# A vision-transformer block on one core: half of a pair's embedding one step ahead, the front part's pieces one slot up, the stores spread, and the last expert in plain products

## The reference

```python
h = _L0_tok_ref(x, L0_tok_W, L0_tok_b)                       # patches (768) @ W.T + b + position
h = concatenate([cls_tok, h], axis=1)                         # 197 tokens
h = h + _L0_attn_ref(_layernorm(h), w_qkv, w_out, b_out)      # 16 heads of 16
h = h + _L0_ffn_ref(_layernorm(h), W1, b1, W2, b2, Wu, bu)

# attention weights: s = p(logits - row maximum), s / sum(s), p a rational function
# the experts (4, hidden size 1024), each token s:
u = sigmoid(x @ Wu + bu);  k = clip(ceil(u * 4), 1, 4)
y = relu(x @ W1[e] + b1[e]) @ W2[e] + b2[e]                   # for every e
out = sum over i = 1..4 of (u / i if k >= i else 0) * y[(s + i - 1) % 4]
```

## Time and profile before

| what | value |
| --- | --- |
| median of 3 runs | 4080.23 us (4076.17 to 4082.94) |
| the profiled execution | 4075.9 us, of which 4074.1 us are the span of its trace |
| PE busy | 3943.3 us, 97% |
| DVE, ACT, POOL busy | 2770.1, 2396.5, 2648.0 us |
| share of the chain that ended last | PE 74%, DVE 12%, issue 4%, DMA 4% |
| transfers | 407.50 MB, mean 100 GB/s |

### The profile page before, as it was taken

One profiled execution on the slowest core, in us unless ns is written; L12 is line 12 of the kernel. 1 busy time (PEld: TensorE's weight loads), 2 busy tenths in 40 slices (PEclk: granted clock), 3 DMA queues, 4 the chain that ended last, 5 costly groups with the idle time before them and its releaser, 6 DMA issues.

```text
span 4074.1 us, 84992 instructions
## 1 busy us (share of the span) xinstructions
PE 3943.3 (97%) x29760; PEld 3331.0 (82%) x29760; DVE 2770.1 (68%) x4223; ACT 2396.5 (59%) x4361; POOL 2648.0 (65%) x3437
## 2 busy tenths in 40 slices
PE   7899999999999999999999999999999999999997
PEld 4688888888888888888888888888888888888887
DVE  5666767667767667676667666677776676766752
ACT  5555566655666555666555665556665556655562
POOL 5466666656667666666566666666665666666677
PEclk8899999999999999999999999999999999999999
DMA  6233333333333333333333333333333333333333
GB/s 193 61 98 99 97 101 99 95 105 83 106 101 102 97 100 96 102 99 98 101 92 99 101 101 99 103 91 102 99 100 101 97 98 102 101 95 90 97 108 94
DMA packets 693839, 407.50 MB, mean 100 GB/s; under 512 B 149169, under 2 KB 684081, under 8 KB 692401
## 3 DMA queue, kind: packets, MB, share of 16 engines
q1 hardware_dynamic: 690400, 401.98, 34.7%
q10 hardware_dynamic: 3024, 0.09, 0.0%
HBM read 384.79 MB, written 17.10 MB: 99 GB/s over the span
## 4 chain that ended last, share of the span: by engine, by line
PE 74%; DVE 12%; issue 4%; DMA 4%; ACT 2%; POOL 2%; SPq 1%; DVEq 0%; ACTq 0%; POOLq 0%
PE ps L1148 45%; PE ps L1278 6%; PE ps L1246 5%; PE ps L1319 4%; PE ps L1231 4%; DMA w1s<-w_sums 4%; PE ps L1260 3%; DVE probs L843 2%; PE ps L1336 2%; DVE lows L916 2%; PE ps L1328 1%; DVE rt L887 1%; DVE rden L863 1%; DVE rstd L889 1%; ACT probs L611 1%
## 5 line engine op out<-in xcount | busy, mean ns | idle before, releaser
L1148 PE MATMUL ps<-xn,w1s 128*128 128x197 f32 x4096 | 903.1, 342 | 4.9 <-ACT hT L576 2.6
L1148 PE MATMUL ps<-hT,w_s 128*128 128x197 f32 x4096 | 790.4, 330 | 9.8 <-POOL hT L474 8.1
L1148 PEld LDWEIGHTS ps<-xn,w1s 128*128 128x128 f32 x4096 | 677.2, 189 | 138.7 <-issue 134.6
L1148 PEld LDWEIGHTS ps<-hT,w_s 128*128 128x128 f32 x4096 | 696.6, 190 | 13.3 <-issue 8.9
L474 POOL TENSOR_TENSOR hT<-hT 128x197 f32<-128x197 f32 x512 | 311.4, 608 | 608.1 <-ACT hT L591 603.2
L1148 PE MATMUL ps<-xt,w1s 128*128 128x197 f32 x3072 | 686.2, 332 | 18.8 <-DMA w1s<-w_sums 17.7
L843 DVE SCALAR_TENSOR_TENSOR probs<-probs,ps 99x788 f32<-99x788 f32 x512 | 481.1, 971 | 307.7 <-ACT probs L611 307.7
L467 POOL TENSOR_SCALAR hT<-hT 128x394 f32<-128x394 f32 x512 | 620.2, 1211 | 20.1 <-DVE hT L958 20.1
L1148 PEld LDWEIGHTS ps<-xt,w1s 128*128 128x128 f32 x3072 | 533.9, 189 | 105.9 <-issue 45.2
L916 DVE TENSOR_REDUCE lows<-ps 99x8 f32<-99x1576 f32 (+1 forms) x256 | 460.4, 1799 | 229.2 <-PE ps L1246 229.2
L1148 PE MATMUL ps<-hT,w_a 128*128 128x197 f32 x3072 | 601.5, 330 | 0.7 <-DVE yw L976 0.7
(11 more groups left out here) (113 smaller groups left out, 5945.8 us busy)
## 6 DMA issues: line engine op xcount, KB each, us to landing
w_a<-in_w SPq DMA_DIRECT2D x384, 256.0 KB, 3.1
w1s<-w_sums SPq DMA_DIRECT2D x512, 192.0 KB, 2.6
w1s<-in_w SPq DMA_DIRECT2D x512, 128.0 KB, 2.4
x<-in_xT SPq DMA_DIRECT2D x30, 1188.0 KB, 5.4
w1s<-in_w SPq DMA_DIRECT2D x512, 64.0 KB, 2.0
w1s<-w_sums SPq DMA_DIRECT2D x512, 64.0 KB, 2.0
out_rows<-rows SPq DMA_DIRECT2D x256, 48.0 KB
hT<-in_w SPq DMA_DIRECT2D x8, 1024.0 KB, 8.6
```

Source lines behind the costliest of these rows:

```text
L1148: return mm(place, weights, rows, start=start, stop=True, skip_group_check=True)
```

## The change

Five things are changed together.

1. **Half of the embedding one step ahead.** `embed(f, 0)` moves to the end of the step before, behind `gate_logit`, and `z` goes from bank 0 to bank `Y1`.
2. **The front's pieces one slot up.** On PE: `embed(f, 1)` in slot 0, `mean` in slot 1, `variance` in slot 2, q and k in slots 4 and 5, v in slot 6. On POOL: `sum_h` in slot 0 and `sum_squares` in slot 2. On ACT and DVE the pieces that go with them move too, and the order of `log_of`, `halves`, `whole`, `normal`, `up_sums_1` and `refine` around them is another. `weigh` goes to other gaps.
3. **The gate's reciprocal in two halves** (`sigmoid`, `sigmoid_2`), and `gate_sum` before the last `low`.
4. **Stores**: three in each of slots 8 to 11, behind the weights of the slot, in place of twelve in slot 9 before them.
5. **The end**: the last expert's down product is done in 16 plain products of 394 columns (`final_products`), with the weight block `a21` loaded to the free pixel buffer; DVE weighs, adds and transposes each half (`final_rows`), and SP and ACT store them by halves, 16 transfers.

```diff
@@ SP
-                    if s == 9 and has_t:
-                        store(t)
...
+                    if n == LAST and s == 8:
+                        sp.wait_ge(emb_done, 2 * PAIRS)
+                        sp.dma_start(a21[:], w2[E - 1][:, 0:COUPLES, P:2 * P]).then_inc(a21_in, 16)
+                    if 8 <= s < 12 and has_t and t < LAST:
+                        store(t, s - 8)
@@ POOL
-                    if s == 1 and has_f:
+                    if s == (1 if f == 1 else 0) and has_f:
                         sum_h(f)
-                    if s == 3 and has_f:
+                    if s == (3 if f == 1 else 2) and has_f:
                         sum_squares(f)
@@ ACT
                 relus(1)
+                if has_f:
+                    h_of(f, 0)
                 for k in range(8):
...
+                    if k == 3 and has_f:
+                        rs_of(f)
...
-                    if k in (0, 1) and has_f:
-                        h_of(f, k)
+                    if k == 0 and has_f:
+                        h_of(f, 1)
...
-                    if k == 2 and has_f:
+                    if k == 1 and has_f:
                         squares(f)
@@ DVE
+                    if k == 2 and has_f:
+                        spread(f, "var", var_done, vt_ready)
                     late(k)
+                    if k == 1 and has_f:
+                        centre(f)
                     if k == 1 and has_n:
                         sigmoid(n)
+                    if k == 2 and has_n:
+                        sigmoid_2(n)
...
+                    if k == 3 and has_f:
+                        refine(f, rs_ready, nt_ready, ht_ready, rstd_ready)
+                        normal_rows(f)
+                    if k == 3:
+                        even(4)
@@ PE
                 if has_b:
-                    gap(b, 0, (low_ready, at(b, 8, 8)), (zb_ready, at(n, 1, 1)), (q_max_ready, at(b, 4, 4)))
+                    gap(b, 0, (low_ready, at(b, 8, 8)), (zb_ready, at(n, 1, 1)), (q_max_ready, at(b, 4, 4)), *([(h_ready, at(f, 2, 1))] if has_f else []))
                 experts(1)
                 if has_f:
-                    embed(f, 0, read(1))
+                    embed(f, 1, read(1))
...
-                    embed(f, 1, read(3))
+                    mean(f, read(3))
...
-                    mean(f, read(5))
+                    variance(f, read(5))
...
                 if has_b:
-                    gate_logit(b, (low_ready, at(f, 8, 8)) if has_f else (vt2_ready, at(b, 1, 1)))
+                    gate_logit(b, (whole_ready, at(b, 8, 8)))
+                if pair + 2 < PAIRS:
+                    embed(pair + 2, 0, (low_ready, at(f, 8, 8)))
+
+            def final_products():
+                pe.wait_ge(a21_in, 16)
+                pe.wait_ge(poly_ready, at(PAIRS, 16, 0))
+                for m in range(DK):
+                    for g in range(COUPLES):
+                        c = FINAL * COUPLES + g
+                        pe.wait_ge(r1_ready, c + 1)
+                        mm(final_y(m), (w_a[:, 0, g], a21[:, g])[m], hidden(c), start=g == 0, stop=False)
+                        pe.wait_ge(r2_ready, c + 1)
+                        if g == 0:
+                            pe.wait_ge(wa_in[(1, 2)[m]], 16 * PAIRS * E)
+                        ins = mm(final_y(m), w_a[:, (1, 2)[m], g], hidden2(c), start=False, stop=g == COUPLES - 1)
+                    ins.then_inc(final_done, 1)
```

More of the change, by code:

```diff
@@ L317, in vit_block, with final_y, store_last @@
         STORES = 4 * (DK + 1)
+        LAST_STORES = 4 * DK * 2
+        FINAL = PAIRS * E - 1
+        a21 = x[:].rearrange("p a k s -> p (a k s)")[:, 0:COUPLES * P].rearrange("p (g c) -> p g c", g=COUPLES)
+        def final_y(m):
+            return ps[:, m, 0:N]
+        def store_last(eng, a, m):
+            eng.wait_ge(rows_ready, LAST + 1 + m)
+            to = out[LAST * N:(LAST + 1) * N, m * P + 32 * a:m * P + 32 * a + 32]
+            full = (NB - 1) * 32
+            eng.dma_start(to[0:full].rearrange("(j n) c -> n j c", n=32),
+                          rows[32 * a:32 * a + 32, m, 0:full].rearrange("p (j c) -> p j c", c=32)).then_inc(rows_out, 16)
+            eng.dma_start(to[full:N], rows[32 * a:32 * a + N - full, m, full:NROW]).then_inc(rows_out, 16)
         block = ctx.enter_context(nc.Block())
@@ L330, in store @@
                 full = (NB - 1) * 32
[L331 to L335, removed]
+                for m in range(DK):
+                    sp.dma_start(to[0:full, a, m, :].rearrange("(j n) c -> n j c", n=32),
+                                 rows[32 * a:32 * a + 32, m, 0:full].rearrange("p (j c) -> p j c", c=32)).then_inc(rows_out, 16)
+                sp.dma_start(to[full:N, a], rows[32 * a:32 * a + N - full, :, full:NROW]).then_inc(rows_out, 16)
             def load_x_part(c):
@@ L776, in step @@
                         square(b, k, 1)
-                    if k in (5, 7) and has_b:
-                        halves(b, (k - 3) // 2)
+                    if k in (6, 7) and has_b:
+                        halves(b, k - 5)
                     if k == 0 and has_n:
@@ L824, in _ @@
             run_steps(step)
+            for m in range(DK):
+                for a in range(2, 4):
+                    store_last(act, a, m)
         @block.vector
@@ L986, in y_weighted, with final_rows @@
                                                op0=ALU.add, op1=ALU.mult).then_inc(yw_ready, 1)
+            def final_rows():
+                dve.wait_ge(gate, at(LAST, 9, 9))
+                dve.wait_ge(rows_out, STORES * 16 * LAST)
+                for m in range(DK):
+                    part = h2[:, LAST % 2, m, 0:N]
+                    dve.wait_ge(final_done, m + 1)
+                    dve.wait_ge(y_ready, at(FINAL, 2, 0))
+                    nc.vector.scalar_tensor_tensor(out=two(yw[:, m, :]), in0=two(final_y(m)), scalar=b2s[:, E - 1, m:m + 1], in1=weight_of(E - 1),
+                                                   op0=ALU.add, op1=ALU.mult).then_inc(final_ready, 1)
+                    dve.wait_ge(final_ready, 2 * m + 1)
+                    nc.vector.tensor_tensor(part, part, yw[:, m, :], ALU.add).then_inc(final_ready, 1)
+                    dve.wait_ge(final_ready, 2 * m + 2)
+                    nc.vector.transpose(rows[:, m, :], h2[:, LAST % 2, m, :]).then_inc(rows_ready, 1)
             def rows_of_pair(t):
@@ L1080, in step @@
                         poly(b, k, 0)
-                    if k in (5, 7) and has_b:
-                        whole(b, (k - 3) // 2)
+                    if k in (6, 7) and has_b:
+                        whole(b, k - 5)
+                    if k in (3, 4, 7):
+                        odd_up(k)
                     if has_b:
                         poly(b, k, 1)
-                    odd(k)
+                    if k not in (3, 4, 7):
+                        odd_up(k)
+                    odd_down(k)
```

139 lines of the change are left out of this document (72 added, 67 removed).

## The result

The changed kernel takes 4059.86 us (median of 5 runs, 4052.97 to 4061.1), the kernel before 4080.23 us in the same session (5 runs, 4076.08 to 4082.94): a ratio of 0.9953, 95% interval 0.9942 to 0.9964. That is 20 us less, where I had forecast 43. The direction is right and the time lies inside the range, but in the part of it that belonged to rival B.

What follows compares the result with a forecast made beforehand. PE, busy 97% of the span, was taken as the floor, leaving its idle time to win. Steps 72.9 - 39.9 = 33.0 us plus end 7.6 gave 40.6 us; median 4039.6, forecast 4037 us, range 4020 to 4052 (chance 0.50).

Steps and rivals of the forecast that it cites:

- rival B: DVE or ACT becomes late in slots 3 to 7: 4052 to 4067, say 4060 us; chance 0.17.
- What the steps lose: PE's waits in the 30 full steps that the change takes away, together 72.9 us.
- The weights: PE's wait for slot 2's weights, queued behind the pixels: all 22.5 us go, with nothing in their place.
- The waits for `poly` and for the last `low`: PE's waits at the q and k projections, 33.9 us, and at the last transposes, 10.8 us: both gone.
- the terms put at nothing for the gate, `weigh`, v and the stores: Moved pieces in slots 4 to 7 and SP's stores: no chain meets PE, 0 us, ends -3 and +15.
- Gap 0: PE waits there for `h_of(f, 0)` on ACT: 0.13 us a step, 3.9 us lost.
- `sum_h` ahead of `y_added`: POOL's slot 0: `y_added` just in time for ACT's copy of a down product, 0 us lost.
- Rival D: Slower: `sum_h` holds up `y_added`, ACT's copy and the variance chain; about 4097 us at 2 us a step; chance 0.06.
- The variance: PE's `variance` product waits for POOL's `sum_squares`: 1.0 us a step, 30 us lost, ends 0 and 1.6 per step.
- Slot 3 on DVE: `refine` and normalisation stand ahead of `up_sums_2`: 0.2 us a step, 6 us lost, ends 0 and 0.6 per step.
- The paragraph on the Trainium skill: Slot 3's moved DVE operations could each stand still for one of POOL's: gain 10 to 20 us smaller.
- The end: Last expert's plain products and half stores, to the end of the span: 7.6 us gained, ends 4 and 9.

Runs made afterwards that it cites:

- alone gave 23: Kernel before, with the next pair's pixels (`load_x`) issued behind slot 2's weights on SP instead of ahead of them: 4052.89 us, 0.9937.
- both later moves: Kernel after, with POOL's `sum_squares` ahead of `relu_2` and DVE's `up_sums_2` ahead of `normal_rows`: 3995.52 us, 0.9790 of before.
- taken away, it gave 1.14: Kernel after, with POOL's `sum_squares` in slot 2 moved ahead of `relu_2`: 4022.8 us, 0.9862 of before.
- order changed: Kernel after, with DVE's `up_sums_2` in slot 3 moved between `refine` and `normal_rows`: 4031.64 us, 0.9881 of before.
- POOL cut: Kernel after, with POOL's `y_added(x, 1)` of slot 3 and `hidden_sums` of slot 4 cut to two columns in full steps: 4021.45 us, 0.9857 of before.
- two single-line swaps: Kernel after, with `sum_squares` put ahead of `relu_2` on POOL and `up_sums_2` ahead of `normal_rows` on DVE: together 3995.52 us.

## Why the forecast was half right

*What the steps lose.* Right in its sum. The weights were forecast at 22.5 us and alone gave 23 (30 steps of 0.77). The waits for `poly` and for the last `low` are gone. With both later moves the step is 2.57 us shorter than before (124.21 to 121.64), 77 us in 30 steps. The forecast had 72.9 less 3.9 for gap 0, or 69. No wait of PE is left then that comes back in every step, so the terms put at nothing for the gate, `weigh`, v and the stores were right.

*Gap 0.* Right: its 16 passes start at 1619.79, the last ones before them at 1619.22 with 0.33 us of work. That is 0.24 us, where 0.09 is usual at a change of shape; 0.15 us against 0.13.

*`sum_h` ahead of `y_added`.* Right at 0 us, and with room: the order doesn't matter at all. Rival D rested on a margin of 0.1 us at ACT's copy. The chain to the variance runs over ACT's relu, which POOL waits for in either order, by 2.8 and 3.8 us.

*The variance.* Right: forecast 1.0 us a step, 0.8 printed, 30 times. Read 0.82 and 27.8 us in all; taken away, it gave 1.14. The chain is the one that was counted: from gap 1 (1629.55), `sum_squares` ends at 10.94 us, where the forecast had 10.95.

*Slot 3 on DVE.* This is the step that failed, 0.2 us a step where it was 1.2 in the trace, and 1.0 (order changed) to 1.14 (POOL cut) in the runs: 30 to 34 us instead of 6. The chain was the right one and was named; its durations were those that the same instructions had elsewhere, where POOL stood still. The row with 0.79 was in the text and became only an upper end of 0.6 us, and the operation behind it, beside POOL too, was left out:

```profile
1665.13 0.76 DVE L889 SCALAR_TENSOR_TENSOR rstd<-rt,rstd 128x394 f32<-128x394 f32 x1
```

With 1.15 us more for the four instructions, the same count gives 1.35 us. The paragraph on the Trainium skill estimated 10 to 20 us, without rows for it, and I left it outside the sum. It was right in kind and still too small. That this is because POOL has five operations without a pause here is my reading; no run varied their number.

*The end.* 4.5 us instead of 7.6. From the end of the Strassen products to the end of the span it is 20.7 us (4038.08 to 4058.8), where I had 18.8 (4047.7 to 4066.5) and before it was 26.4. The wait of 2.4 us was forecast (2.7), and so were the three operations on DVE (2.0 us, measured 1.95). The product that waits and the three behind it cost 1.8 us more than at full clock, and that was not forecast. The last 1.2 us are lost ahead of this place: from the last `gate_logit` to the first plain product the kernel after takes 92.3 us, and the kernel before 91.1 to the same place. That is the lower clock behind the wait for POOL (3.0 us lost instead of 1.6). So the forecast had the work of the end right and left out the clock: where it stayed at 1.00 behind `w_a`, the same end gained 7.4 and 7.6 us. What decides the clock at either place stays open.

*The sum.* Forecast 69.0 - 36 = 33.0 us in the steps. Measured 77.1 - 64.2 = 12.9 (30 x 0.43): 28 us more were put in place than forecast (24 of them in slot 3 on DVE and 4 at the variance), and 8 more taken away.

Rival B is what happened, for the reason that it gave ("the margins there are small") and at the upper end of its price. Its counter, that 30% of DVE is idle, says nothing about a queue of five instructions in front of one that PE wants.

## What to carry to other kernels

When instructions are moved between engines' queues, take their durations with the neighbours that they will have. If DVE's read two SBUF operands and GpSimd is busy then, count both as standing still by turns, or put the one that PE waits for first. A moved group goes behind the instruction that is wanted next, unless someone waits for the group sooner; here two single-line swaps were worth three times the whole change. And behind a wait of PE of some us, look at the granted clock: the wait can be charged twice, once itself and once at the lower clock, though two kernels here had the wait and not the lower clock.

## What the hardware showed that I had not expected

- A GpSimd subtraction on two columns took 0.94 us beside a DVE multiplication of 0.98 us on SBUF operands, and 0.20 us beside `up_sums_2`. `up_sums_2`, with one operand in PSUM and one in SBUF, kept its 0.56 us with POOL's subtraction of 1.22 us beside it.
- After 2.4 to 2.5 us without work, PE ran 4.4 us at a mean granted clock of 0.61 in five kernels, which cost 1.8 us, and at 1.00 in two; without the gap it stayed at 1.00 in the same place.
- Taking the wait at the variance away gave more than the wait: 1.14 us a step for 0.98. What the rest is stays open.
